# Attention kernel: row sums of the probabilities folded to 64 rows and taken with one matmul instead of two

## The reference

```python
xr = x.reshape(B, C, S).transpose(0, 2, 1)
qkv = (xr @ w_qkv + b_qkv).reshape(B, S, N_HEADS, 3 * d_k)
q, k, v = jnp.split(qkv, 3, axis=-1)
attn = jnp.einsum('bihd,bjhd->bijh', q, k) * scale
attn = jax.nn.softmax(attn, axis=2)
out = jnp.einsum('bijh,bjhd->bihd', attn, v).reshape(B, S, N_HEADS * d_k)
out = out @ w_proj + b_proj
out = out.transpose(0, 2, 1).reshape(B, C, H, W)
return out + x
```

## Time and profile before

| | us |
|---|---|
| median of 2 runs | 3987.8 (3986.29 to 3989.31) |
| the profiled execution, its own time | 3987.98 |
| its span | 3985.9 |
| TensorE matmuls busy | 3936.3 |
| VectorE busy | 3319.5 |
| GpSimd busy | 3006.5 |
| ScalarE busy | 2935.8 |

### The profile page before, as it was taken

One profiled execution on the slowest core, in us unless ns is written; L12 is line 12 of the kernel. 1 busy time (PEld: TensorE's weight loads), 2 busy tenths in 40 slices (PEclk: granted clock), 3 DMA queues, 4 the chain that ended last, 5 costly groups with the idle time before them and its releaser, 6 DMA issues.

```text
span 3985.9 us, 60063 instructions
## 1 busy us (share of the span) xinstructions
PE 3936.3 (99%) x18464; PEld 3360.4 (84%) x18464; DVE 3319.5 (83%) x4449; ACT 2935.8 (74%) x5529; POOL 3006.5 (75%) x2371
## 2 busy tenths in 40 slices
PE   8999999999999999999999999999999999999998
PEld 6878888888888888888888888888888888888886
DVE  7788888888888888888888888888888888888887
ACT  5777777777777777777777777777777777777775
POOL 4678777777777777777777777877778777787775
PEclk9999999999999999999999999999999999999999
DMA  6344444434443344443444444444344434444432
GB/s 201 85 108 112 125 107 110 118 95 132 110 120 104 99 131 112 111 113 96 132 105 127 107 107 111 116 128 107 95 121 112 129 100 108 112 110 127 113 93 79
DMA packets 262943, 451.23 MB, mean 113 GB/s; under 512 B 107872, under 2 KB 118112, under 8 KB 258656
## 3 DMA queue, kind: packets, MB, share of 16 engines
q1 hardware_dynamic: 262624, 447.39, 42.4%
HBM read 204.48 MB, written 41.42 MB: 62 GB/s over the span
## 4 chain that ended last, share of the span: by engine, by line
PE 89%; issue 4%; DVE 4%; ACT 2%; DMA 1%; POOL 0%; SPq 0%; ACTq 0%; DVEq 0%
PE ps_g L473 24%; PE s L495 11%; PE ps_o L517 11%; PE ps_o L515 11%; PE st L574 11%; PE st L572 10%; PE ps_g L489 9%; DVE acc L806 2%; PE st L501 1%; PE st L502 1%; ACT p_hl L731 1%; ACT x_h L690 1%; ACT p L728 0%; DVE acc L803 0%; DVE qk_l L787 0%
## 5 line engine op out<-in xcount | busy, mean ns | idle before, releaser
L963 POOL TENSOR_TENSOR p_hl<-p,p_hl 128x512 fp32r<-128x512 f32 x2048 | 2609.0, 1298 | 915.0 <-ACT p_hl L731 914.4
L728 ACT ACTIVATE p<-st 128x512 f32<-128x512 f32 x2048 | 1231.8, 601 | 705.3 <-PE st L574 678.5
L809 DVE TENSOR_REDUCE nm<-s 128x1 fp32r<-128x1024 f32 x1024 | 1250.1, 1221 | 381.6 <-PE s L495 370.8
L806 DVE TENSOR_TENSOR acc<-acc,p 128x512 f32<-128x512 f32 x1792 | 1234.1, 689 | 25.5 <-DVE acc L803 0.5
L731 ACT ACTIVATE p_hl<-st 128x512 fp32r<-128x512 f32 x2048 | 1237.7, 604 | 0.0
L515 PE MATMUL ps_o<-p_hl,v_hl 128*128 128x512 f32 x2048 | 802.9, 392 | 4.5 <-POOL p_hl L963 3.9
L574 PE MATMUL st<-q,k 128*128 128x512 f32 x2048 | 804.4, 393 | 0.0
L517 PE MATMUL ps_o<-p_hl,v_hl 128*128 128x512 f32 x2048 | 802.0, 392 | 0.0
L572 PE MATMUL st<-q,k 128*128 128x512 f32 x2048 | 799.6, 390 | 1.4 <-DVE v_hl L794 1.1
L473 PE MATMUL ps_g<-x_h,wq 128*128 128x512 f32 x2016 | 711.5, 393 | 6.4 <-DVE qk_l L787 6.3
L495 PE MATMUL s<-k,q 128*128 128x512 f32 x2048 | 646.7, 396 | 9.0 <-DMA k<-qk_l 4.7
(11 more groups left out here) (192 smaller groups left out, 3756.8 us busy)
## 6 DMA issues: line engine op xcount, KB each, us to landing
k<-qk_h SPq DMA_DIRECT2D x256, 256.0 KB, 4.3
wq<-wq_d SPq DMA_DIRECT2D x126, 512.0 KB, 4.5
ring<-x_in SPq DMA_DIRECT2D x128, 256.0 KB, 3.7
q<-qk_h SPq DMA_DIRECT2D x128, 256.0 KB, 3.8
q<-qk_l SPq DMA_DIRECT2D x128, 256.0 KB, 4.9
k<-qk_l SPq DMA_DIRECT2D x128, 256.0 KB, 5.1
q<-q SPq DMA_DIRECT2D x256, 128.0 KB, 4.9
rinv<-rinv_d SPq DMA_DIRECT2D x256, 128.0 KB, 2.9
```

The costliest lines, as they stand in the source:

```text
L728: nc.scalar.activation(p[:, to, :], st[slot % RING][:], ACT.Exp)
L806: nc.vector.tensor_tensor(acc[:], acc[:], probs, ALU.add).then_inc(acc_done, 1)
L809: nc.vector.tensor_reduce(nm[:, it:it + 1], s1[:], AXX, ALU.max, negate=True).then_inc(max_done, 1)
L963: nc.gpsimd.tensor_tensor(p_l[:, to, :], p[:, to, :], p_h[:, to, :].bitcast(f32), ALU.subtract).then_inc(pl_done, 1)
```

## The change

It works on the row sums alone. In code, line numbers being those of the kernel before:

- `acc_h`, `acc_l` and their two matmuls go. ScalarE copies rows 64 to 127 of `acc` into `fold` (`copy_fold`), VectorE adds rows 0 to 63 to it (`finish_half`), ScalarE writes the high part of `fold` into rows 0 to 63 of `fold_hl` (`high_fold`, between the exps of tile 0 and tile 1 of a unit with U % 4 == 1), VectorE writes the low part into rows 64 to 127 (`low_fold`), and one matmul of `fold_hl` with ones sums all 128 rows.
- The copy of tile 0 and the addition of tile 1 of a half's first unit become one addition of two SBUF tiles into `acc`, behind the maximum of the unit with U % 4 == 1. `low_fold` follows it.
- The sums move on TensorE from the unit with U % 4 == 1 to the next one; ScalarE's taking of the row, the store of the sums, their load and the inverse move with them, the last to the start of the unit with U % 4 == 1, the load to the start of U % 4 == 0 on SP's queue.

```diff
@@ -86,11 +86,11 @@
             return per * self.b + i if per * self.b + i > 0 else None
 
         def slot(self, unit, e):
-            sums = (unit + 2) // 4
+            sums = (unit + 1) // 4
             return 2 * unit + e + (max(1, sums) if self.first and unit >= 0 else sums)
 
         def sum_slot(self, half):
-            return self.slot(4 * half + 5, 1) + 1
+            return self.slot(4 * half + 6, 1) + 1
 
         def group(self, unit):
 
...
@@ -363,6 +365,10 @@
                 b, at = B.b, B.at
                 for U in range(UNITS):
                     h, u = divmod(U, IT)
+                    if U % 4 == 0 and B.on(half := (U - 8) // 4, HALVES):
+                        n = half % 2
+                        sp.wait_ge(row_stored[n], at(16 * HEADS, 16 * (half // 2 + 1)))
+                        load_sums(n)
                     if u == 0:
                         if (v := at(SLOTS, B.slot(U - 1, 1) + 1)) is not None:
                             sp.wait_ge(st_done, v)
@@ -394,13 +400,9 @@
                     if u == 7 and B.on(h + 1, HEADS):
                         sp.wait_ge(max_stored[0], at(16 * HEADS, 16 * (h + 2)))
                         load_max(0)
-                    if U % 4 == 2 and B.on(half := (U - 6) // 4, HALVES):
+                    if U % 4 == 3 and B.on(half := (U - 7) // 4, HALVES):
                         sp.wait_ge(st_free, at(SLOTS, B.sum_slot(half) + 1))
                         store_sums(half)
-                    if U % 4 == 3 and B.on(half := (U - 7) // 4, HALVES):
-                        n = half % 2
-                        sp.wait_ge(row_stored[n], at(16 * HEADS, 16 * (half // 2 + 1)))
-                        load_sums(n)
                     if U % 4 == 1 and B.on(half := (U - 9) // 4, HALVES):
                         n = half % 2
                         sp.wait_ge(recip_done, at(HALVES, half + 1))
...
@@ -497,9 +501,8 @@
                 return mm
 
             def sums(bank, halves):
-                pe.wait_ge(accl_done, halves)
-                nc.tensor.matmul(bank[:], ones[:], acc_h[:], start=True, stop=False)
-                nc.tensor.matmul(bank[:], ones[:], acc_l[:], start=False, stop=True).then_inc(st_done, 1)
+                pe.wait_ge(foldl_done, halves)
+                nc.tensor.matmul(bank[:], ones[:], fold_hl[:], start=True, stop=True).then_inc(st_done, 1)
 
             def weighted_values(B, unit):
                 at = B.at
@@ -626,7 +629,7 @@
                         held = ("bias", 0)
                     if U == 1 and B.first:
                         pe.wait_ge(vl_done, V0)
-                    if U % 4 == 1 and B.on(half := (U - 5) // 4, HALVES):
+                    if U % 4 == 2 and B.on(half := (U - 6) // 4, HALVES):
                         slot = B.sum_slot(half)
                         pe.wait_ge(st_free, at(SLOTS, slot - 2))
                         sums(st[slot % RING], at(HALVES, half + 1))
@@ -676,6 +679,15 @@
                     act.wait_ge(norm_done, v)
                 nc.scalar.copy(tmp[rows, half % 2, :], ps_o[other, :]).then_inc(half_moved, 1)
 
+            def copy_fold(halves):
+                if halves is not None:
+                    act.wait_ge(foldl_done, halves)
+                nc.scalar.copy(fold[:], acc[D:P, :]).then_inc(fold_copied, 1)
+
+            def high_fold(halves):
+                act.wait_ge(fold_done, halves)
+                nc.scalar.copy(fold_hl[0:D, :], fold[:]).then_inc(foldh_done, 1)
+
             def take_row(half, bank):
 
                 rows, _ = half_rows(half)
@@ -729,6 +741,8 @@
                         if e == 0 and (v := at(UNITS, U - 1)) is not None:
                             act.wait_ge(pv_done, v)
                         nc.scalar.activation(p_h[:, to, :], st[slot % RING][:], ACT.Exp).then_inc(st_free, 1)
+                        if e == 0 and U % 4 == 1 and B.on(half := (U - 5) // 4, HALVES):
+                            high_fold(at(HALVES, half + 1))
                     kind, i, e = B.group(U)
                     if kind == "qk" and e == 1:
                         head, n = divmod(i, 2)
@@ -751,8 +765,8 @@
                         nc.scalar.activation(wp[0][:, k, :], wp_stage[:, k, :], ACT.Copy).then_inc(wp_high, 1)
                     if U % 4 == 0 and B.on(half := (U - 4) // 4, HALVES):
                         act.wait_ge(acc_done, at(2 * UNITS, 8 * half + 8))
-                        nc.scalar.copy(acc_h[:], acc[:]).then_inc(acch_done, 1)
-                    if U % 4 == 1 and B.on(half := (U - 5) // 4, HALVES):
+                        copy_fold(at(HALVES, half))
+                    if U % 4 == 2 and B.on(half := (U - 6) // 4, HALVES):
                         slot = B.sum_slot(half)
                         act.wait_ge(st_done, at(SLOTS, slot + 1))
                         take_row(half, st[slot % RING])
...
@@ -795,26 +810,34 @@
                                         v[:, :, :, 0:D].bitcast(f32), ALU.subtract).then_inc(vl_done, 1)
 
             def add_probs(B, unit, e):
-                probs = p[:, unit % 2 * 2 + e, :]
+                probs = [p[:, unit % 2 * 2 + i, :] for i in range(2)]
+                if unit % 4 == 0 and e == 0:
+                    return
                 dve.wait_ge(st_free, B.at(SLOTS, B.slot(unit, e) + 1))
-                if unit % 4 == 0 and e == 0:
+                if unit % 4 == 0:
+
                     if (v := B.at(HALVES, unit // 4)) is not None:
-                        dve.wait_ge(accl_done, v)
-                    nc.vector.tensor_copy(acc[:], probs).then_inc(acc_done, 1)
+                        dve.wait_ge(fold_done, v)
+                    nc.vector.tensor_tensor(acc[:], probs[0], probs[1], ALU.add).then_inc(acc_done, 2)
                 else:
                     dve.wait_ge(acc_done, B.at(2 * UNITS, 2 * unit + e))
-                    nc.vector.tensor_tensor(acc[:], acc[:], probs, ALU.add).then_inc(acc_done, 1)
+                    nc.vector.tensor_tensor(acc[:], acc[:], probs[e], ALU.add).then_inc(acc_done, 1)
 
             def maximum(it):
                 nc.vector.tensor_reduce(nm[:, it:it + 1], s1[:], AXX, ALU.max, negate=True).then_inc(max_done, 1)
 
             def finish_half(half, halves):
                 rows, _ = half_rows(half)
-                dve.wait_ge(acch_done, halves)
-                nc.vector.tensor_tensor(acc_l[:], acc[:], acc_h[:].bitcast(f32), ALU.subtract).then_inc(accl_done, 1)
+                dve.wait_ge(fold_copied, halves)
+                nc.vector.tensor_tensor(fold[:], acc[0:D, :], fold[:], ALU.add).then_inc(fold_done, 1)
                 dve.wait_ge(half_moved, halves)
                 nc.vector.tensor_tensor(tmp[rows, half % 2, :], ps_o[rows, :], tmp[rows, half % 2, :],
                                         ALU.add).then_inc(half_done, 1)
+
+            def low_fold(halves):
+                dve.wait_ge(foldh_done, halves)
+                nc.vector.tensor_tensor(fold_hl[D:P, :], fold[:], fold_hl[0:D, :].bitcast(f32), ALU.subtract
+                                        ).then_inc(foldl_done, 1)
 
             def invert(n, loads):
                 dve.wait_ge(s64_loaded[n], loads)
@@ -871,6 +894,8 @@
                 b, at = B.b, B.at
                 for U in range(UNITS):
                     h, u = divmod(U, IT)
+                    if U % 4 == 1 and B.on(half := (U - 9) // 4, HALVES):
+                        invert(half % 2, at(16 * HEADS, 16 * (half // 2 + 1)))
                     if U % 4 == 1 and B.on(half := (U - 5) // 4, HALVES):
                         finish_half(half, at(HALVES, half + 1))
                     if B.on(unit := U - 1, UNITS):
@@ -883,8 +908,8 @@
                         maximum(it)
                     if B.on(unit := U - 1, UNITS):
                         add_probs(B, unit, 1)
-                    if U % 4 == 0 and B.on(half := (U - 8) // 4, HALVES):
-                        invert(half % 2, at(16 * HEADS, 16 * (half // 2 + 1)))
+                    if U % 4 == 1 and B.on(half := (U - 5) // 4, HALVES):
+                        low_fold(at(HALVES, half + 1))
                     if U in X_SPLIT and B.ahead and X_SPLIT[U] not in X_POOL:
                         c = X_SPLIT[U]
                         k, n = c % KT, c // KT
...
```

More of the change, by code:

```diff
@@ L148, in attention_kernel @@
         rinv = sb("rinv", [P, NH, HALF])
-        acc_h = sb("acc_h", [P, HALF], f32r)
-        acc_l = sb("acc_l", [P, HALF], f32r)
+        fold = sb("fold", [D, HALF])
+        fold_hl = sb("fold_hl", [P, HALF], f32r)
         ones = sb("ones", [P, P], f32r)
@@ L221, in attention_kernel @@
         acc_done = sem("acc_done")
-        acch_done = sem("acch_done")
-        accl_done = sem("accl_done")
+        fold_copied = sem("fold_copied")
+        fold_done = sem("fold_done")
+        foldh_done = sem("foldh_done")
+        foldl_done = sem("foldl_done")
         row_stored = [sem(f"row_stored{i}") for i in range(NH)]
@@ L445, in _ @@
             bodies(body)
```

(6 more changed lines are left out.)

## The result

The changed kernel takes 4336.5 us (median of 2 runs, 4333.2 to 4339.8) against 3987.8: 1.0873 times the time before, 95% interval 1.0856 to 1.0891. It is slower by 349 us; 332 had been forecast.

What follows compares the result with a forecast made beforehand. The prediction took TensorE's steps and waits to bound the kernel: 3988 - 59 for removed matmuls + 389 for waits at ps_g = 4318, stated as 4320 us, 8.3% slower; range 3990 to 4380.

Steps and rivals of the forecast that it cites:

- What bounds the kernel: TensorE's steps plus its waits; the tight meeting with VectorE is bank ps_g, slack 0.45 us once per half.
- The matmul removed: On TensorE, 256 matmuls go at a step of 0.23 us each, so 59 us come off.
- The deadline moves 0.45 us: TensorE reaches the next unit's ps_g group 0.45 us earlier, spending the whole slack there.
- The joint addition and the low part: Both VectorE instructions read two SBUF tiles, wait for GpSimd's running one, and have means near 1.0 and 1.7 us.
- GpSimd's tile 1 would go between them: GpSimd's tile 1 is ready before the joint addition ends and goes ahead of low_fold, which ends at 2121.88 in unit 29.
- 4068: Time in us if low_fold goes ahead of GpSimd's tile 1, with a wait of 0.57 us per half; chance 0.11.
- rival 2: No exclusion between GpSimd and the joint addition or low_fold; TensorE waits at most 0.25 us, 3929 to 3990; chance 0.10.
- The price of a wait: At ps_g in unit 29, TensorE waits 1.49 us plus 0.11 for slower first matmuls: 1.60 us, taken for all halves.
- the loosest and the tightest: Ends of halves in an image, units 57 and 45, with waits for ps_g priced at 1.37 and 2.14 us.
- The count: Of 256 halves some 243 pay the wait, as some groups are missing in the first and last image: 389 us.
- Hidden work: GpSimd's waits for VectorE, twice per half, some 0.55 us each, are hidden; ScalarE's 256 more short copies add 154 us.
- waits for the load of the sums: VectorE's late inverse at the unit's start, costed at nothing; as a rival, 1 us more every half, near 4575; chance 0.04.

Runs made afterwards that it cites:

- spare copy: The changed kernel with one more 64 x 512 ScalarE copy of fold, behind the high part and ahead of tile 1's exps: 4155.3 us, ratio 1.0424.
- the low part behind the read: The changed kernel with low_fold moved behind VectorE's read of ps_g in units with U % 4 == 1: 3993.8 us, ratio 1.0017.
- the low part from PSUM: The changed kernel with low_fold reading acc (PSUM) in place of fold (SBUF), for timing alone: 4108.6 us, ratio 1.0307.

## Why the prediction was right

- **What bounds the kernel.** The steps of TensorE and its waits, and `ps_g` as the meeting point that is tight: right. TensorE's idle time against reads of `ps_g` went from 12.6 to 326 us.
- **The matmul removed.** 0.23 us each was forecast, 0.227 measured from the units' lengths. By busy time it would have been 0.39.
- **The deadline moves 0.45 us.** Right: TensorE is free for the group 5.03 us into unit 29's time (2300.68 - 2295.65), where 2121.21 - 2116.16 = 5.05 was forecast. That move alone costs 38 us, 37 were worked out before its run.
- **The joint addition and the low part.** Forecast 1.0 and 1.7 us, measured 1.01 and 1.65. In unit 29 the forecast times from the unit's start were 4.01 and 5.72 for their ends; they ended at 4.00 and 5.69. That GpSimd's tile 1 would go between them was the step that decided between 4320 and 4068; it went first in 253 of 256 halves, and when it was held back (spare copy) the time fell. Moving one operand of each to PSUM took 310 us away, which settles rival 2.
- **The price of a wait.** 1.60 forecast from unit 29, 1.58 measured behind it in the same image. For the loosest and the tightest of that image the forecasts were 1.37 and 2.14 (the steps given add up to 2.11), and 1.28 and 1.99 came out. That the mean of images 1 to 14 is 1.596 is partly luck: without the seven falls of the clock, for which the prediction has no term, it would be 1.55.
- **The count.** The term that was mis-sized: 243 halves. The profiled execution is 345 us longer than before, where the forecast's terms make 389 - 59 = 330. Images 1 to 14 account for 224 x 1.369 = 307 us, as forecast, so the first and last image bring 38 us in 32 halves, 1.2 a half, nearly as much as the others. The forecast's 19 waits there make 23. Groups missing there did not spare the wait as I had assumed: 28 of these 32 units with U % 4 == 2 are 0.9 us or more longer than before. That is the 15 us.
- **Hidden work.** GpSimd's subtractions became longer (2609.0 to 2698.6 us busy, 0.35 us a half, where some 0.55 twice was forecast), and ScalarE has its copies; in images 1 to 14 neither shows in the length of any unit but those that wait for `ps_g`. VectorE's waits for the load of the sums are 6.5 us in all. The added work is not free in general: in the versions where the read waits no longer, units 6 and 22 wait for just these engines.

The Trainium skill's rule ("SBUF — State Buffer", "Who interferes with whom") that a VectorE instruction with two SBUF inputs and a GpSimd instruction reading SBUF exclude each other held in every form tried: 64 rows or 128, output in SBUF or PSUM, and not with one input in PSUM. That issue order decides who blocks, which the prediction took from the same section, agrees with the 253 of 256 halves here, but not with the places in the last section, where the measurement decides.

What stays open: how the 59 us divide that are left with no exclusion and beyond the earlier deadline, what decides whether the clock falls behind a wait, and when GpSimd keeps VectorE out for more than one instruction (below).

## What to carry to other kernels

Price a removed matmul by its step, not its busy time, and ask first how much slack TensorE has at the next bank it waits for: work that it no longer does brings that wait closer by as much. On VectorE, put what TensorE waits for ahead of what nobody waits for, but follow each moved instruction to its own taker; the two reads moved ahead here gave their gain back one or two groups later. An elementwise instruction of VectorE with both inputs in SBUF costs a GpSimd instruction's rest on top when GpSimd is busy; one input in PSUM avoids it, at no price here (684 ns with it, 0.68 us at the shortest without).

## What the runs showed of the hardware beyond that

VectorE and GpSimd mostly take turns, but not always. In the run with the spare copy, unit 5 of image 8, VectorE's joint addition (two SBUF inputs) was issued while GpSimd ran, and waited for three of GpSimd's instructions, the one that ran and two more. VectorE, then GpSimd:

```profile
2106.16 4.09 DVE L825 TENSOR_TENSOR acc<-p 128x512 f32<-128x512 f32 x1
2110.28 0.68 DVE L843 TENSOR_TENSOR fold_hl<-fold,fold_hl 64x512 fp32r<-64x512 f32 x1
```

```profile
2105.95 1.28 POOL L1004 TENSOR_TENSOR os_hl<-o,os_hl 128x512 fp32r<-128x512 f32 x1
2107.20 2.49 POOL L993 TENSOR_TENSOR p_hl<-p,p_hl 128x512 fp32r<-128x512 f32 x2
2111.50 2.51 POOL L993 TENSOR_TENSOR p_hl<-p,p_hl 128x512 fp32r<-128x512 f32 x2 [1.80 <-ACT p_hl L747]
```

GpSimd's last one ended at 2109.69 and VectorE's 0.56 later; GpSimd's own had their usual length. It happened to the joint addition 11 times in 256 in that run, once in the changed kernel (3.24 us), once with the low part behind the read and twice with the low part from PSUM, always in unit 5. It happened to the low part 6 times, always with TensorE in unit 6, in the run that has it behind the read and the copy and addition of before. Each time it was three instructions, up to where GpSimd had to wait for ScalarE.

In unit 5 of images 3, 5, 6 and 12 of the run with the spare copy it went the other way: VectorE's joint addition was issued 0.22 to 0.30 us after the start of GpSimd's instruction, went first (0.68 us), and GpSimd's took 2.1 us. In the 11 cases it was 0.21 to 0.27 us after. So the order of issue alone does not decide it, and what does is not shown. Unit 6 behind such a case is 9.1 to 10.0 us long, 5.3 in those four images; in all 11 the granted clock also fell to half there, for 3.4 us or 6.8.
